# Linear attention and routed layers: the router's mask compares with the logits in PSUM, rank digits come from one rounding, the gates' product runs on GpSimd

## The reference, cut to what matters

```
logits = x @ gate_w.T
topk_w, topk_idx = top_k(softmax(logits), 4)
topk_w = topk_w / sum(topk_w)
order = argsort(e_flat)
pos = arange(t * K) - starts[e_s]
slot = minimum(pos, C)
buf = zeros((E, C + 1, h)).at[e_s, slot].set(x[t_s])
```

## Time and profile before

| | us |
|---|---|
| median of 3 runs | 1836.39 |
| lowest and highest | 1835.27, 1837.31 |
| the profiled execution: its own time | 1833.1 |
| the profiled execution: its span | 1831.4 |
| TensorE busy in the span | 1437.3 (78%) |
| VectorE busy | 1405.0 (77%) |
| GpSimd busy | 1383.8 (76%) |
| ScalarE busy | 975.1 (53%) |

### The profile page before, as it was taken

How to read it: one execution, slowest core, us unless ns; L and a number is a source line. 1 busy time by engine, 2 the same in 40 slices (tenths; PEclk the granted TensorE clock), 3 DMA queues, 4 the chain that set the end, 5 groups by cost and what they waited for, 6 DMA issues and landing times.

```text
span 1831.4 us, 23737 instructions
## 1 busy us (share of the span) xinstructions
PE 1437.3 (78%) x5979; PEld 864.0 (47%) x6020; DVE 1405.0 (77%) x2764; ACT 975.1 (53%) x1676; POOL 1383.8 (76%) x962
## 2 busy tenths in 40 slices
PE   5777843435898889888998899888975898999980
PEld 3665643322343344433443344333433666988770
DVE  3898851111999999999999999999997476568884
ACT  2555520103656665566646665566652466877760
POOL 2554464762999999999999999999893577647776
PEclk8989865557999999999999899899998899999995
DMA  5333359433223322233123322233311322545553
GB/s 149 111 93 90 90 156 238 63 38 105 94 86 122 134 93 95 84 127 133 59 86 122 133 76 81 109 133 114 106 77 48 113 74 86 154 127 157 158 139 83
DMA packets 201422, 198.62 MB, mean 108 GB/s; under 512 B 22664, under 2 KB 180296, under 8 KB 197064
## 3 DMA queue, kind: packets, MB, share of 16 engines
q1 hardware_dynamic: 178568, 172.09, 28.9%
q0 software_dynamic: 22784, 25.71, 7.1%
HBM read 138.31 MB, written 61.90 MB: 109 GB/s over the span
## 4 chain that ended last, share of the span: by engine, by line
PE 36%; DVE 23%; issue 13%; POOL 7%; DMA 3%; ACT 2%; DVEq 2%; POOLq 0%; SPq 0%; another core or an unknown queue 0%; ACTq 0%
PE bank L1271 12%; DVE hst L1645 12%; PE bank L1226 6%; POOL dbx L778 2%; DVE prod L1661 2%; PE bank L1387 2%; PE bank L1377 2%; PE bank L1364 2%; PE bank L1361 2%; PE bank L1388 2%; PE bank L1224 2%; POOL yg L839 1%; PE bank L1260 1%; PE bank L1284 1%; DVE st L1442 1%
## 5 line engine op out<-in xcount | busy, mean ns | idle before, releaser
L778 POOL TENSOR_TENSOR dbx<-u,ball 128x1024 f32<-128x1024 f32 x256 | 614.2, 2501 | 5.7 <-POOL u L809 2.8
L1645 DVE TENSOR_TENSOR_SCAN hst<-bank,dbx 128x512 f32<-128x512 f32 x512 | 591.7, 1204 | 8.6 <-POOL dbx L778 4.1
L1271 PE MATMUL bank<-prod,ident 128*128 128x512 f32 x1024 | 511.1, 636 | 20.0 <-DVE prod L1661 14.8
L982 ACT ACTIVATE bank<-dt,aneg 128x511 f32<-128x511 f32 x512 | 346.3, 688 | 277.0 <-DVE hst L1645 274.6
L1271 PEld LDWEIGHTS bank<-prod,ident 128*128 128x128 f32 x1024 | 206.0, 204 | 258.2 <-issue 208.2
L1661 DVE TENSOR_TENSOR prod<-hst,bank 128x1024 f32<-128x1024 f32 x192 | 233.4, 1216 | 17.2 <-DVE hst L1645 13.8
L787 POOL TENSOR_TENSOR prod<-hst,call 128x1024 f32<-128x1024 f32 x64 | 161.3, 2520 | 22.4 <-DVE hst L1645 22.3
L839 POOL DMA_INDIRECT yg<-expert_rows,row_of x128 | 126.9, 991 | 58.9 <-issue 35.5
L1255 PE MATMUL bank<-parts,sel_c 128*128 128x512 bf16 x152 | 60.6, 400 | 76.5 <-DVE prod L1661 75.8
L1226 PE MATMUL bank<-x2T,inc 128*128 128x512 f32 x256 | 116.7, 599 | 0.0
L827 POOL DMA_INDIRECT sorted_rows<-x3b,row_of x80 | 78.6, 982 | 28.4 <-issue 25.1
(11 more groups left out here) (287 smaller groups left out, 2905.5 us busy)
## 6 DMA issues: line engine op xcount, KB each, us to landing
ball<-b_rows SPq DMA_DIRECT2D x32, 2048.0 KB, 7.1
call<-b_rows SPq DMA_DIRECT2D x16, 1024.0 KB, 9.5
xr<-sorted_rows SPq DMA_DIRECT2D x48, 256.0 KB, 4.0
expert_rows<-yu SPq DMA_DIRECT2D x48, 256.0 KB, 2.5
xg_rows<-xg SPq DMA_DIRECT2D x16, 320.0 KB, 3.0
xt<-in_x SPq DMA_DIRECT2D x16, 256.0 KB, 3.0
xT<-in_xT SPq DMA_DIRECT2D x16, 256.0 KB, 3.5
resid_rows<-zero SPq DMA_DIRECT2D x16, 256.0 KB, 3.6
```

The source lines that it names most:

```text
L778: gp.tensor_tensor(dbx[n % NDB][:, :, :], u[s.par][:, :, :], ball[:, n:n + 1, :].to_broadcast([P, NH, SEQ]), ALU.mult).then_inc(dbx_rdy, 1)
L982: act.activation(da_ps[h][:, 1:SEQ], dt_[s.par][:, h, 1:SEQ], ACT.Exp, scale=aneg[:, h, n:n + 1]).then_inc(da_rdy, 1)
L1271: last = mm(y_ps[:, h, :], ident[:, :], from_[:, h, :], start=False, stop=(n == NS - 1), skip_group_check=True)
L1645: dve.tensor_tensor_scan(h_of[:, h, :], da_ps[h][:, :], dbx[n % NDB][:, h, :], 0.0, ALU.mult, ALU.add).then_inc(scan_rdy, 1)
```

## The change

- `mask` reads its second operand from `gu_ps` in PSUM in place of `lg` in SBUF. `lg` stays, for the maxima and `match_replace`. TensorE's next write of `gu_ps` waits for the mask in place of `hsh`.
- The upper digit `rka` is now the rank less 3.5, rounded to a multiple of eight by adding and subtracting one large number in one instruction, and `rkb` is the difference of `rnk` and `rka`. `rkt` is gone. The constants follow: `iota_a` counts in eights, `iota_b` is shifted by 3.5, and `carry` starts 3.5 lower. GpSimd makes two constants more before the others may start.
- The gates' product moves from VectorE to GpSimd, between the reciprocal root and the digits. VectorE's next write of `gm` waits for it, and SP stores `xg` behind it. `route0` has 14 steps per sequence now and `rank0` 4.
- The order of everything else is the same.

```
-N_EARLY = 15
+N_EARLY = 17
...
+MAGIC_8 = 100663296.0
+MIDDLE = SLOT_B / 2 - 0.5
...
-                sp.wait_ge(route0, s.at(15, 15))
+                sp.wait_ge(gates_rdy, s.at(1, 1))
+                settle(sp)
+                sp.wait_ge(x1_rdy, s.at(TT, TT))
                 sp.dma_start(xg_d[bass.ds(s.at(SEQ), SEQ), :].rearrange("(t p) d -> p t d", p=P), xg[s.par][:, :, :]
...
-            make(gp.iota(iota_e[:, :], [[1, E0]], base=0, channel_multiplier=0, allow_small_or_imprecise_dtypes=True))
+            make(gp.iota(iota_a[:, :], [[SLOT_B, SLOT_A]], base=0, channel_multiplier=0, allow_small_or_imprecise_dtypes=True))
+            make(gp.iota(iota_b[:, :], [[1, SLOT_B]], base=0, channel_multiplier=0, allow_small_or_imprecise_dtypes=True))
+            make(gp.tensor_scalar(iota_b[:, :], iota_b[:, :], MIDDLE, None, ALU.subtract))
...
-                gp.wait_ge(rank0, s.at(6, 6))
+                gp.wait_ge(rank0, s.at(4, 4))
                 need(gp, ohb_rdy, s.at(1))
                 settle(gp)
-                digit_off(dgb, rkb, SLOT_B, dg_rdy)
+                digit_off(dgb, rkb, iota_b, SLOT_B, dg_rdy)
...
-                digit_off(dga, rka, SLOT_A, dg_rdy)
+                digit_off(dga, rka, iota_a, SLOT_A, dg_rdy)
...
+            def gates_of(s):
+                gp.wait_ge(route0, s.at(14, 14))
+                need(gp, st_xg[s.par], s.half(16))
+                settle(gp)
+                gp.tensor_tensor(xg[s.par][:, :, D:XGW], gm[:, :, :], gr[:, :].rearrange("p (t e) -> p t e", e=1).to_broadcast([P, TT, E0]),
+                                 ALU.mult).then_inc(gates_rdy, 1)
...
                 for i in (2, 3):
                     rsqrt(rstd, mv, Seq(j, i), mv_rdy, rstd_rdy)
+                    gates_of(Seq(j, i - 1))
                     slots_of(Seq(j, i - 1))
...
-                    need(pe, rank0, r.at(6, -4))
+                    need(pe, rank0, r.at(4, -2))
...
-                    need(pe, hsh_rdy, r.at(1))
+                    need(pe, route0, r.at(14, -3))
                     for k in range(TT):
                         last = mm(gu_ps[:, k, 0:GW], x1T[:, tile(k)], wcat[:, :], start=True, stop=True)
...
-            dve.memset(carry[:, :], BIG).then_inc(dve_init, 1)
+            dve.memset(carry[:, :], BIG - MIDDLE).then_inc(dve_init, 1)
...
-                    tt(mask[:, :, :], rep[:, :, :], lg[:, :, :], ALU.not_equal).then_inc(route0, 1)
+                    tt(mask[:, :, :], rep[:, :, :], gu_ps[:, :, 0:E0], ALU.not_equal).then_inc(route0, 1)
...
                     dve.wait_ge(lexp_rdy, r.at(1, 1))
+                    need(dve, gates_rdy, r.at(1))
                     tt(gm[:, :, :], lexp[:, :, :], mask[:, :, :], ALU.mult).then_inc(route0, 1)
...
                     dve.reciprocal(gr[:, :], gs[:, :]).then_inc(route0, 1)
-                    dve.wait_ge(route0, r.at(15, 14))
-                    tt(xg[r.par][:, :, D:XGW], gm[:, :, :], col(gr, E0), ALU.mult).then_inc(route0, 1)
...
-                    dve.wait_ge(rank0, r.at(6, 2))
-                    ts(rkt[:, :], rnk[:, :], 1.0 / SLOT_B, 0.5 / SLOT_B - 0.5, ALU.mult, ALU.add).then_inc(rank0, 1)
-                    dve.wait_ge(rank0, r.at(6, 3))
-                    ts(rkt[:, :], rkt[:, :], MAGIC, None, ALU.add).then_inc(rank0, 1)
-                    dve.wait_ge(rank0, r.at(6, 4))
                     need(dve, dg_rdy, r.at(2))
-                    ts(rka[:, :], rkt[:, :], MAGIC, None, ALU.subtract).then_inc(rank0, 1)
-                    dve.wait_ge(rank0, r.at(6, 5))
-                    stt(rkb[:, :], rka[:, :], -float(SLOT_B), rnk[:, :], ALU.mult, ALU.add).then_inc(rank0, 1)
+                    ts(rka[:, :], rnk[:, :], MAGIC_8, MAGIC_8, ALU.add, ALU.subtract).then_inc(rank0, 1)
+                    dve.wait_ge(rank0, r.at(4, 3))
+                    tt(rkb[:, :], rnk[:, :], rka[:, :], ALU.subtract).then_inc(rank0, 1)
```

More of the change, by code:

```diff
@@ L157, in build @@
         restart = {n: sb(f"restart{n}", [P, E1, n * TT]) for n in sorted(set(BATCH))}
-        iota_e = sb("iota_e", [P, E0])
+        iota_a = sb("iota_a", [P, SLOT_A])
+        iota_b = sb("iota_b", [P, SLOT_B])
         neghalf = sb("neghalf", [P, TT])
@@ L221, in build @@
             rnk = eb("rnk", [P, TT * E0])
-            rkt = eb("rkt", [P, TT * E0])
             rka = eb("rka", [P, TT * E0])
@@ L361, in build @@
         tg_rdy, sg_rdy, hsh_rdy = sem("tg_rdy"), sem("sg_rdy"), sem("hsh_rdy")
-        lexp_rdy = sem("lexp_rdy")
+        lexp_rdy, gates_rdy = sem("lexp_rdy"), sem("gates_rdy")
         d_mm, mt_mm = sem("d_mm"), sem("mt_mm")
@@ L653, in _, with digit_off @@
                                   pattern=[[-SLOT_B, SLOT_A], [1, P]], channel_multiplier=-1))
-            def digit_off(dst, digit, width, done):
+            def digit_off(dst, digit, values, width, done):
                 a = digit[:, :].rearrange("p (k w) -> p k w", w=1).to_broadcast([P, TT * E0, width])
-                b = iota_e[:, 0:width].rearrange("p (k w) -> p k w", k=1).to_broadcast([P, TT * E0, width])
+                b = values[:, :].rearrange("p (k w) -> p k w", k=1).to_broadcast([P, TT * E0, width])
                 gp.tensor_tensor(dst[:, :, :], a, b, ALU.subtract).then_inc(done, 1)
             def slots_of(s):
-                gp.wait_ge(rank0, s.at(6, 6))
+                gp.wait_ge(rank0, s.at(4, 4))
                 need(gp, ohb_rdy, s.at(1))
                 settle(gp)
-                digit_off(dgb, rkb, SLOT_B, dg_rdy)
+                digit_off(dgb, rkb, iota_b, SLOT_B, dg_rdy)
                 need(gp, oha_rdy, s.at(1))
@@ L683, in _ @@
                     rsqrt(rstd, mv, Seq(j, i), mv_rdy, rstd_rdy)
+                    gates_of(Seq(j, i - 1))
                     slots_of(Seq(j, i - 1))
+            gates_of(Seq(0, NB - 1))
             slots_of(Seq(0, NB - 1))
@@ L691, in _ @@
                          allow_small_or_imprecise_dtypes=True))
-            for mask in restart.values():
-                make(gp.memset(mask[:, :, :], 1.0))
-                make(gp.memset(mask[:, :, 0:1], 0.0))
+            for ramp in restart.values():
+                make(gp.memset(ramp[:, :, :], 1.0))
+                make(gp.memset(ramp[:, :, 0:1], 0.0))
             make(gp.memset(sel_c[:, :, :], 0.0))
@@ L875, in stage1 @@
                     act.wait_ge(gu_mm, r.at(1, 1))
-                    need(act, route0, r.at(15))
+                    need(act, route0, r.at(14))
                     act.activation(lg[:, :, :], gu_ps[:, :, 0:E0], ACT.Copy
@@ L889, in stage1 @@
                 if r:
-                    act.wait_ge(route0, r.at(15, 5))
-                    need(act, route0, r.at(15))
+                    act.wait_ge(route0, r.at(14, 5))
+                    need(act, route0, r.at(14))
                     act.activation(lexp[:, :, :], lsub[:, :, :], ACT.Exp).then_inc(lexp_rdy, 1)
@@ L1143, in stage1 @@
                     last.then_inc(d_mm, 1)
-                    pe.wait_ge(route0, r.at(15, 11))
+                    pe.wait_ge(route0, r.at(14, 11))
                     chosen = mask[:, :, :].rearrange("p t e -> p (t e)")
@@ L1484, in stage1 @@
                         dve.max(top[:, k, :], lg[:, k, :]).then_inc(route0, 1)
-                    dve.wait_ge(route0, r.at(15, 4))
+                    dve.wait_ge(route0, r.at(14, 4))
                     dve.wait_ge(tg_rdy, r.at(1, 1))
@@ L1492, in stage1 @@
                     tt(hsh[:, :, :], sg[:, :, :], gu_ps[:, :, E0 + I0:GW], ALU.mult).then_inc(hsh_rdy, 1)
-                    dve.wait_ge(route0, r.at(15, 6))
+                    dve.wait_ge(route0, r.at(14, 6))
                     settle(dve)
@@ L1522, in stage1 @@
                 if r:
[L1523 removed]
+                    dve.wait_ge(route0, r.at(14, 12))
                     dve.tensor_reduce(gs[:, :], gm[:, :, :], AX.X, ALU.add).then_inc(route0, 1)
[L1525 removed]
+                    dve.wait_ge(route0, r.at(14, 13))
                     dve.reciprocal(gr[:, :], gs[:, :]).then_inc(route0, 1)
[L1527 to L1528 removed]
                     dve.wait_ge(d_mm, r.at(1, 1))
@@ L1534, in stage1 @@
                        carry[:, :].rearrange("p (t e) -> p t e", t=1).to_broadcast([P, TT, E0]), ALU.add).then_inc(rank0, 1)
-                    dve.wait_ge(rank0, r.at(6, 1))
+                    dve.wait_ge(rank0, r.at(4, 1))
                     tt(carry[:, :], carry[:, :], tot_ps, ALU.add).then_inc(rank0, 1)
```

13 lines of the change are left out of this document (3 added, 10 removed).

## The result

The changed kernel takes 1821.11 us (median of 4 runs, 1817.65 to 1824.31), the kernel before 1835.86 in the same comparison. The recorded ratio is 0.9909, 95% interval 0.9886 to 0.9931: 16.7 us faster, 1819.7 on the 1836.39 shown first, just under the low end of the range I gave and 7.7 us under the forecast. The two medians alone are 14.8 us apart (0.9920), which lies inside the interval; the forecast of 1827.4 lies outside it (1815.5 to 1823.7). The direction was right, the size was not. The change repeated in a second comparison at 0.9895 [0.9864, 0.9925].

The account below looks back on a forecast made before the run. Layer 0's routing was bound by a chain through VectorE and GpSimd, with late logits in some periods. 6 × 1.23 + 8 × 0.14 + 0.5 gave 9.0 us, so 1827.4 from the median 1836.4; range 1820 to 1834.

Parts of the forecast that it names:

- The mask: Layer 0 routing: mask falls to 0.29 us, gm inherits the wait; 0.57 of 1.43 us kept, nothing with late logits.
- `gm` above 1 us in fast periods: Sign in the routing trace: gm, inheriting the wait for GpSimd, lasts over 1 us where the logits are on time.
- my sum of a fast period: Routing period with logits on time: 0.57 + 0.52 + 0.14 = 1.23 us saved, giving 12.98.
- The digits: Rank digits on VectorE: two of four instructions go, 0.52 us off the chain, nothing in a period with late logits.
- The product: Gates' product on GpSimd takes 0.48 us until 172.12; normalise waits for it, so 0.14 of 0.31 us is kept.
- The period: Length of a routing period after the change: 12.98 us with logits on time, 14.07 with logits late.
- three things that I had named as proof against me: Routing signs: late-logits period gone, normalise waiting over 0.2 us, or gm not stalling.
- The count: Routing periods with late logits: 5/9 of 14, so 8 late saving 0.14 us each and 6 fast saving 1.23.
- closes the first gap and leaves the second: TensorE idle time: the 1.04 us ahead of the k/v projection goes, the 2.22 us ahead of the transposes stays.
- all periods fast: Rival for the routing: TensorE's clock stays up, 14 × 1.23 + 0.5 = 17.7 us, 1818.7; chance 0.14.
- The end of the stage: Behind the routing's last sequence: the shorter digits save 0.5 us.
- can only shift: Stages behind layer 0's routing: no changed computation, so they start earlier, everything shifted by the same 9 us.

Follow-up runs that it names:

- three digits: Changed kernel with one more digit instruction on VectorE's chain (three instead of two); ratio 0.9921 to the kernel before.
- the fillers: Unread TensorE products added ahead of the transposes: six in the changed kernel 0.9889, six in the kernel before 1.0015, four in the changed kernel with gm later 0.9857.
- the last experiment: Changed kernel plus an unread 2048-element sum on VectorE between the routing and the later stages; ratio 0.9903 to the kernel before.

## Why the prediction was right or wrong

**The mask** was right in place and size: 0.288 us on the mean, 0.58 kept of its 1.43, the rest inherited by `gm`, which stopped 0.15 us behind `dga` as the old mask had. Moving `gm` shows that the inheritance need go no further. The sign "`gm` above 1 us in fast periods" came with the mask alone (1.25 us) and not in the changed kernel (0.73 to 0.85): there VectorE first waits 0.29 us for `lg`, a term that my sum of a fast period did not have, and comes to `gm` that much later behind the start of `dga`. Since `gm` waits for `dga` anyway, this costs nothing. By the section on the TRN2 errata in the Trainium skill's "VectorE: DVE Perf Modes", `mask` would have been an estimated 65 ns dearer with its PSUM source; the trace shows 288 ns for it beside the 0.29 us of an SBUF pair, no difference.

**The digits** were priced at 0.52 and are worth 0.45 alone.

**The product** was undervalued, by the step that let it last until 172.12 and normalise wait for 0.17. It takes 0.40 us and not 0.48, and it starts 0.03 ahead of the recorded end of the `pow` and not 0.08 behind it. Those two make 0.19 us, a little more than the whole wait. The mechanism is real, as the product made twice shows, but the single one ends in time. It keeps 0.26 of 0.31, where I gave it 0.14. The GPSIMD Engine Reference of the Trainium skill, "Engine selection", puts GpSimd at about half VectorE's speed for such work: the trace has 0.40 us against 0.29, 1.4 times and not twice, and since it ends in time even that costs the chain nothing.

**The period.** None of the three things that I had named as proof against me came: late periods remain, normalise doesn't wait, `gm` stalls. On time 12.83 against a forecast of 12.98, late 13.4 to 14.1 against 14.07. An on-time period has lost 1.41 us instead of 1.23: 11 × 0.18 = 2.0 us.

**The count** is the step that failed most. "I take 5/9 of 14, 8 late" turned nine gaps and five late products into a share per gap, and applied it to all fourteen periods because the change "closes the first gap and leaves the second". The gaps came out much as forecast (0.16 and 1.9 us); the share did not. Three were late, so five more periods gained 1.23 instead of 0.14: 5 × 1.09 = 5.5 us. Together with the 2.0 that makes 7.5, and with the forecast's 8.5 it gives 16.0 for the fourteen periods, where 15.0 were measured; the last period holds a wait of 2.40 us (next paragraph). The trace of before held a warning: the earlier trace rows show a gap of 2.22 us followed by an on-time product, and I never asked what told the four such periods from the five late ones. The rule cannot be mended by a better fraction, since mask alone (gap 2.2 us) has none late and three digits (1.9 us) five. What sets the count stays open: the fillers show that idle time of TensorE is needed in the changed kernel, and neither gap nor the idle time as a whole orders the kernels. The rival "all periods fast", 1818.7, came nearest; its reason, that one gap closes, isn't enough, since three periods stay late, and that the measured time lies 1 us from it owes something to luck (next paragraphs).

**The end of the stage.** I gave it 0.5 us. It comes 3.4 us sooner after the last transposes (22.35 us instead of 25.71 to the start of `lx`), for a reason that I had not seen. In the kernel before, VectorE sits for 5.32 us ahead of the last list sum, for the last 3.34 of which TensorE has finished (its last list product ends at 266.15) and nothing that the profile shows is missing:

```profile
269.49 0.42 DVE L1470 TENSOR_TENSOR lsum<-lsum,bank 128x256 f32<-128x256 f32 x1 [5.32 <-issue]
```

In the changed kernel such a wait comes earlier, in the middle of four maxima, one period before the end:

```profile
223.13 0.29 DVE L1492 MAX8 top<-lg 128x8 f32<-128x32 f32 x2 [2.40 <-issue]
```

The wait moved rather than went: 0.5 us more in the last of the fourteen periods (14.45 against 13.97), 3.4 less behind them. Without it the end would be as long as before (25.71 − 3.34 = 22.37 against 22.35), and the digits' 0.5 is not to be seen. The gain of these 3.4 us was luck, as far as the forecast goes. Against it, the changed kernel reached its second transposes 2.3 us later (47.50 against 45.17); in the fourteen traces these come between 44.4 and 47.5 with no pattern by the number of early constants, which I had costed at nothing. So `lx` starts 15.0 + 3.4 − 2.3 = 16.0 us sooner (253.94 instead of 269.94; the terms are rounded).

**The later stages** "can only shift" was wrong as a statement about one execution: they took 7.0 us more in the first profile, and −4.3 to +6.8 in the twelve others (sum of the table's last two columns, against 1312.1). Which of it lies in the program and which in the one profiled execution, these runs don't tell, though the changed kernel's two executions agree within 0.4 us. By the ratio the kernel gained 16.7 us, about as much as its routing did in the profile.

## What to carry to other kernels

A stall of VectorE behind GpSimd is inherited by the next instruction with two SBUF operands, so price the relief by the release, not by the stall, and look whether that instruction can be moved behind others that don't stall; here that was worth another 0.36 us a period. A count of slow stretches cannot be scaled from the trace of before: find what a slow stretch would have to meet in order to cost something, give the time for none and for all, and let the range reach to each. Filler in a gap of TensorE held the clock up here (0.95 to 0.98), but it brought 3.1 us in fourteen periods only where late logits bound, and none where they did not.

## What the runs showed that I had not expected

- The changed kernel met the slow clock in the same periods twice (late products at 88.57 and 115.29, and at 87.58 and 114.31), and its unchanged routing in the last experiment met it three times as well, but in other periods (111.14, 137.82, 164.61). With 0.29 us more on the chain it was five.
- TensorE idled most in the kernel with the mask alone (56 of the 191 us), and that one had a granted clock of 0.99 and no late period.
- VectorE waits for 2.4 to 3.3 us with no cause that the profile names, once near the end of the routing, in the code that follows the loop. This stands ahead of the last list sum in the kernel before, in the same with fillers and with the mask alone (5.32, 5.30 and 5.28 us of idle time), ahead of the maxima in the changed kernel and the seven made from it with as many digit instructions (2.40 to 2.47), ahead of other instructions with the digits alone and with three digits (2.41, 3.32), and nowhere over 2 us with the product alone. Its place goes with the program; fetching of instructions would fit, and was not tested.
- The state-space stage, the same code in all, took between 878.6 and 885.1 us, for reasons that these runs leave open.
